# Attention in a fused transformer block: bursts of weighings in six sections a head in place of eight

## The reference

```python
attn = jnp.einsum('gqd,gkd->gqk', q, k) * norm      # g: 2 x 16 = 32 heads, q and k: 2048 each
attn = jax.nn.softmax(attn, axis=-1)
ctx = jnp.einsum('gqk,gkd->gqd', attn, v)
```

## Time and profile before

| | |
|---|---|
| median of 3 runs | 3110.65 us (3104.18 to 3110.95) |
| profiled execution | 3103.39 us, span 3101.6 us |
| TensorE (PE) busy | 3064.5 us, 99% |
| VectorE (DVE) busy | 1878.4 us, 61% |
| ScalarE (ACT) busy | 1514.1 us, 49% |
| GpSimd (POOL) busy | 1418.1 us, 46% |
| attention block | 358.6 to 1857 us of the span |

### The profile page before, as it was taken

How to read it: one execution, slowest core, us unless ns; L and a number is a source line. 1 busy time by engine, 2 the same in 40 slices (tenths; PEclk the granted TensorE clock), 3 DMA queues, 4 the chain that set the end, 5 groups by cost and what they waited for, 6 DMA issues and landing times. The chain is left out here.

```text
span 3101.6 us, 41537 instructions
## 1 busy us (share of the span) xinstructions
PE 3064.5 (99%) x15568; PEld 2100.0 (68%) x15568; DVE 1878.4 (61%) x3184; ACT 1514.1 (49%) x2853; POOL 1418.1 (46%) x489
## 2 busy tenths in 40 slices
PE   7999999999999999999999999999999999999998
PEld 5888755555555555555555554778888888888887
DVE  5445988888888888888888874743332322323232
ACT  4333376666666666666666665443222222222221
POOL 2223288888888888888888883000000000000000
PEclk9999999999999999999999999999999999999999
DMA  7666588888888888888888875742211212111111
GB/s 254 195 204 183 153 174 181 181 176 181 180 183 181 178 181 181 181 181 178 182 181 182 181 159 157 278 173 92 72 48 58 75 31 76 45 61 58 48 58 34
DMA packets 149352, 446.40 MB, mean 144 GB/s; under 512 B 26913, under 2 KB 44577, under 8 KB 113954
## 3 DMA queue, kind: packets, MB, share of 16 engines
q0 software_dynamic: 28592, 204.48, 31.9%
q1 hardware_dynamic: 119506, 239.25, 26.0%
q10 hardware_dynamic: 1056, 0.00, 0.0%
HBM read 166.85 MB, written 80.21 MB: 80 GB/s over the span
## 5 line engine op out<-in xcount | busy, mean ns | idle before, releaser
L1272 DVE TENSOR_REDUCE mxp<-pmax 128x1 f32<-128x512 f32 x1968 | 1202.0, 679 | 244.5 <-PE pmax L1047 244.4
L1218 ACT ACTIVATE prob<-pexp 128x512 f32<-128x512 f32 x2023 | 1019.9, 626 | 398.8 <-PE pexp L1096 396.7
L1047 PE MATMUL pmax<-k,q 96*128 96x512 f32 x1968 | 811.8, 413 | 1.1 <-PEq L429 1.1
L1096 PE MATMUL pexp<-q,k 98*128 98x512 f32 x2023 | 804.2, 400 | 0.7 <-ACT prob L1218 0.6
L53 PE MATMUL pproj<-h2f,w 128*128 128x512 f32 x3072 | 717.4, 389 | 0.0
L53 PEld LDWEIGHTS pproj<-h2f,w 128*128 128x128 f32 x3072 | 576.5, 188 | 119.6
L1351 POOL TENSOR_TENSOR gsum<-gsum,prob 128x2048 f32<-128x2048 f32 x127 | 583.7, 4596 | 36.4 <-ACT prob L1218 27.0
L1047 PEld LDWEIGHTS pmax<-k,q 96*128 96x128 f32 x1968 | 374.3, 190 | 280.7 <-DVE mxp L1272 169.3
L1107 PE MATMUL pctx<-prob,v 128*32 128x512 f32 x4096 | 493.4, 598 | 0.0
L1351 POOL TENSOR_TENSOR gsum<-prob 128x2048 f32<-128x2048 f32 x96 | 458.9, 4781 | 31.2 <-ACT prob L1218 31.0
L1891 DVE TENSOR_TENSOR hid<-sil,pproj 128x512 f32<-128x512 f32 x128 | 88.0, 687 | 630.7 <-PE pproj L53 629.1
(11 more groups left out here) (141 smaller groups left out, 1657.9 us busy)
## 6 DMA issues: line engine op xcount, KB each, us to landing
gsum<-prob POOLq DMA_DIRECT2D x187, 1024.0 KB, 7.4
w<-w_scratch SPq DMA_DIRECT2D x128, 256.0 KB, 2.6
q<-q_scratch SPq DMA_DIRECT2D x96, 256.0 KB, 4.5
k<-k_scratch SPq DMA_DIRECT2D x96, 256.0 KB, 6.2
q_scratch<-obq SPq DMA_DIRECT2D x32, 512.0 KB, 5.3
k_scratch<-obq SPq DMA_DIRECT2D x32, 512.0 KB, 3.7
xin<-in_L_attn_query_dram SPq DMA_DIRECT2D x8, 1024.0 KB, 7.9
v_scratch<-vst SPq DMA_DIRECT2D x8, 1024.0 KB, 5.0
```

The lines of the kernel that those rows point to most:

```text
L1047: pe.matmul(pmax[:, bank, :], qst[slot][0:KR, qt * P:(qt + 1) * P], kst[slot][0:KR, kc * TOK:(kc + 1) * TOK], start=True, stop=True).then_ ...
L1096: pe.matmul(score_bank(g, n), kst[slot_of(g)][:, kt * P:(kt + 1) * P], qst[slot_of(g)][:, j * TOK:(j + 1) * TOK], start=True, stop=True).t ...
L1218: act.activation(prob_tile(g, kt)[:, j * TOK:(j + 1) * TOK], score_bank(g, n), ACT.Exp, scale=SCALE).then_inc(exp_done, 1)
L1272: dve.tensor_reduce(mxp[:, par, u // QJ, u % QJ:u % QJ + 1], pmax[:, bank, :], X, ALU.max).then_inc(mx_done, 1)
```

## The change

The sections become unequal: tiles 0 to 2, 3 and 4, 5 to 7, 8 to 10, 11 to 13, 14 and 15, so 12, 8, 12, 12, 12 and 8 pairs of M and q. Six bursts stand behind them: tiles 14 and 15 of the head before; 0 to 2; the two units and tiles 3 and 4; 5 to 7; 8 to 10; 11 to 13. The places of the turn (48), the units (31), the division (8) and the reciprocal (36) by pair stay as they are, and so does the last head's step. The wait for the loads of head g + 2 stays ahead of pair 48.

```diff
-PAIRS = KT // 2
+SECTIONS = ((0, 3), (3, 5), (5, 8), (8, 11), (11, 14), (14, 16))
...
+UNIT_SECTION = [QJ * end - 1 for _, end in SECTIONS].index(UNIT_AFTER)
...
-    own = [[] for _ in range(PAIRS)]
-    late = [[] for _ in range(PAIRS)]
-    for kt in range(KT):
-        b = kt // 2 + 1
-        to = own[b] if b < PAIRS else late[b - PAIRS]
-        to.append(("weigh", kt))
-    late[UNIT_AFTER // 8] += [("unit", k) for k in range(UNITS)]
+    own = [[] for _ in SECTIONS]
+    late = [[] for _ in SECTIONS]
+    for b, (first, end) in enumerate(SECTIONS):
+        to = own[b + 1] if b + 1 < len(SECTIONS) else late[0]
+        to += [("weigh", kt) for kt in range(first, end)]
+    late[UNIT_SECTION] += [("unit", k) for k in range(UNITS)]
...
-                    for b in range(PAIRS):
-                        if b == PAIRS - EARLY // 8 and exists(g + 2):
-                            pe.wait_ge(loaded[slot_of(g + 2)], loads(g + 2))
-                        m = q = 8 * b
-                        for x in ORDER:
-                            if x == "M":
-                                ahead(g, m)
-                                m += 1
-                            else:
-                                score(g, q)
-                                q += 1
+                    for b, (first, end) in enumerate(SECTIONS):
+                        for n in range(QJ * first, QJ * end):
+                            if n == NM - EARLY and exists(g + 2):
+                                pe.wait_ge(loaded[slot_of(g + 2)], loads(g + 2))
+                            ahead(g, n)
+                            score(g, n)
                         if late[b] and exists(g - 1):
                             burst(g - 1, late[b])
                         burst(g, own[b])
...
-                    for b in range(PAIRS):
-                        for n in range(8 * b, 8 * b + 8):
+                    for b, (first, end) in enumerate(SECTIONS):
+                        for n in range(QJ * first, QJ * end):
                             exp(g, n)
                         if exists(g - 1):
                             if b == 0:
                                 read_ctx(g - 1)
-                            if b == UNIT_AFTER // 8:
+                            if b == UNIT_SECTION:
                                 read_sum(g - 1)
```

More of the change, by code:

```diff
@@ L1190, in last_step @@
                         if kt == LAST_UNITS_AT:
-                            burst(LAST - 1, late[UNIT_AFTER // 8])
+                            burst(LAST - 1, late[UNIT_SECTION])
                     finish_tile(KT - 1)
```

## The result

The changed kernel takes 3310.73 us as the median of 5 runs (3305.27 to 3313.07), the kernel before 3110.66 on the same chip. The ratio is 1.065 (95% interval 1.0637 to 1.0663): 200 us slower, where 33 us more were forecast (3144) and 3166 was the upper end of the range. The span of the profiled execution of after is 3310.4 us.

What follows compares the result with a forecast made beforehand. TensorE was taken to bound the attention block, with VectorE at 83% of it. Per head -0.70 + 0.91 + 0.97 = +1.18 us, times 31 heads 36.6, giving 3140, put at 3144 for the median of runs; range 3122 to 3166.

Steps and rivals of the forecast that it cites:

- the sentence on the division: Division at pair 8 of a head, 0.68 us, falls behind reduction 7: costed at nothing, up to 0.6 us without cover.
- Two bursts fewer: TensorE, between sections: fewer bursts of weighing save 0.70 us a head, 0.35 a burst.
- The reductions: VectorE starts one per 0.60 us against 0.47 delivered; waits add 0.25, 0.25 and 0.41 in sections 0, 2, 3: 0.91 a head.
- The turn: Matrix turn after pair 48, now inside section 4, waits for reduction 47 and row maximum: section 7.10 us, net +0.97 a head.
- Faster by 22 us: Rival: bursts' 0.70 saved, no waits because VectorE catches up, 3082 us; against it the 0.60 reduction pitch; chance 0.05.
- The hidden turn: Rival: the turn costs what it does today, reduction waits at their low end; 0.03 us a head, 3104 us; chance 0.07.
- The falling clock: Rival: TensorE's idle wait before the turn lowers its clock, up to 1.7 us a time; 3155 to 3197 us; chance 0.13.

Runs made afterwards that it cites:

- the control: The kernel before with its eight sections, division moved to pair 62 (of head g - 2) and reciprocal to pair 32: 3111.40 us, ratio 1.0004.

## Why the prediction was wrong

The direction was right, the size was not: +200 us for +33. The reasons given for the direction hold, but they make 40 of the 200.

**The step that failed** is the sentence on the division: "I cost it at nothing, because VectorE would be free about 8.4 after the section's start [...]; without that cover it would cost up to 0.6." It took the division for 0.68 us wherever it stands. The runs put in its place: 5.2 us in 27 heads, because it now starts 0.12 to 0.19 us into an addition of GpSimd. With one input from PSUM, at the same place, it is 0.68 and the total 3150. The trace of before had it: its line's maximum is 4178 ns, and the last three divisions (2.98, 4.18 and 1.77 us) lie in additions. The prediction even had the shift that makes them meet, tile 15 ready 1.8 us before the next head's start instead of 0.9, but asked only whether GpSimd's sums would still come in time. It read the division's duration from an ordinary row, and did not ask what the two engines do at the same moment. The Trainium skill has the rule: SBUF — State Buffer, Who interferes with whom, says that a VectorE instruction with two SBUF inputs contends with a GpSimd instruction that reads SBUF, and that the ports they share are held exclusively. The traces agree, 5.2 us for 0.68. It also says that the order of issue decides who blocks. The traces give starts, and by these the order doesn't decide: with the division at pair 0 it waited at a lead of 0.45 us in 24 cases of 27.

**What a meeting costs**, from the sections of after between 1100 and 1400 us: the burst after section 0, with the wait behind it, is 5.06 for 1.85, so 3.21 of standing still. Section 1 takes 5.86, 6.36 or 6.97 in turn, for 3.95. In the head shown, reductions run one after the other from 1245.88; the eighth, which the section's last M needs, would have ended at 1250.76, and the burst could have begun at 1251.47, 4.86 after the first M: 0.91 for the pace of VectorE. The rest, 1.0, 1.5 and 2.1, and 1.07 in a burst of every third head, I put down to the lower clock, 1.9 on average. Together 6.0 us, and 27 times that is 162, for the 161 between the medians of after and of the run with the division at pair 61. The split into pace and clock is worked out from rows; no run took the clock's part alone.

**The other terms of the sum came out.** Two bursts fewer, 0.70: the bursts are 1.85 and 2.71, and sections of 12 without waits 5.85 for 5.83 (half-width reductions). The reductions: 6.13 in sections 0 and 2 is 0.28 over 5.85, for 0.25, and 6.22 in section 3 is 0.37 for 0.41. The turn: 7.05 for 7.10. Net 49.7 a head for 49.6, that is +1.30 for +1.18, and 3149.3 for 3144 in the run at pair 61, whose profiled execution has the one meeting of the bias.

**The rivals.** Faster by 22 us: fell for the reason given. With half-width reductions it came about in part, 0.30 us a head of the 0.70, since the section with the turn still takes 6.4. The hidden turn: fell, 31 waits. The falling clock: the clock did fall, but not where I had put it. Behind the turn's 0.97 us of idle TensorE it stays at 2.4 GHz, with 1.00 granted over the block in the run with the division at pair 61; behind 3.1 us it falls to 1.2, in after each of the 28 times (0.53 in the window above). So the Trainium skill's page TensorE: Matmul & The Clock Gate (A second HAM failure mode: psum-queue depth-cycling) is not borne out for the turn's gaps here. The gap of 1.08 us at the block's start, on which this rival rested, stands in both kernels: in before 0.58 was granted from 360 to 364 us, in after 1.00. Why isn't shown.

One row group needs a word: the earlier trace rows shows the turns from 732.4 us on, 24 of the 31. They give 1113.3 / 23 = 48.4 us a head, the same.

## What to carry to other kernels

When an edit shifts one engine's work against another's, ask of each instruction what the other engine does at that moment, and look at the longest row of its line, not the typical one: an elementwise VectorE instruction with two SBUF inputs is short only where GpSimd pauses. Put such an instruction well ahead of GpSimd's next one (0.69 us was enough here, 0.46 was not), or take one input from PSUM. Before making a producer's runs longer to save its turnovers, work out from pace and number of banks how long a run the consumer can follow (here 10 pairs, nearly without a wait, by 0.60 against 0.47 us and four banks), and keep waits on its last result at the start of a run, not in the middle.

## What was unexpected of the hardware

A VectorE subtraction over one lane was held up as long, 5.83 us, as the multiplication over 128. The multiplication of 0.68 us took up to 5.87 us although the trace has it start 0.45 us before the GpSimd instruction that it then waits for; with a lead of 0.69 us and more none in these traces waited. Between 0.46 and 0.69 there is no row, and below 0.46 the same lead gave both outcomes: of the multiplications 24 of 27 waited at 0.45 and 0.46, the one at 0.37, and 21 of 27 at 0.05 to 0.15. The subtraction, with 0.45 in both, waited in the control and not in the kernel before. A place that misses a pause of 1.15 us by 0.15 us moved a kernel by 5%.
